# A software-pipelined decoder round in another order on TensorE, VectorE and ScalarE

## What is computed

```python
x = x + L1_attn(LN(x))     # RWKV: k, v, r = shifted mixes @ W; wkv scan over 16 steps;
                           # x += (r * wkv) @ Wo; then channel mix:
                           # x + sigmoid(yr @ Wcr) * (relu(yk @ Wck)**2 @ Wcv)
x = x + L1_xattn(LN(x), context)
    # scores = Q K^T (4 heads, 77 keys); keep the 32 largest; softmax; mean over heads
    # c_t = attn_mean @ V; film: x = n*(1+scale_in)+shift_in
    # y = irfft(rfft(x) * Kf); y = y*(1+scale_out)+shift_out; xt = x + y
    # h = gelu(LN(xt) @ W1 + b1) @ W2 + b2;  LN(xt + h)
x = x + clip(LN(x) @ sign(W) * scale + bias, -100, 100)
```

## Time and profile before

| | us |
|---|---|
| median of 3 runs | 1935.76 |
| lowest and highest run | 1935.62, 1937.24 |
| time of the profiled execution | 1936.92 |
| its span, first to last instruction | 1935.2 |
| TensorE busy in the span | 1686.4 (87%) |
| VectorE busy | 1287.0 (67%) |
| ScalarE busy | 864.3 (45%) |
| GpSimd busy | 605.3 (31%) |

### The profile page before, as it was taken

One profiled execution on the slowest core, in us unless ns is written; L12 is line 12 of the kernel. 1 busy time (PEld: TensorE's weight loads), 2 busy tenths in 40 slices (PEclk: granted clock), 3 DMA queues, 4 the chain that ended last, 5 costly groups with the idle time before them and its releaser, 6 DMA issues.

```text
span 1935.2 us, 26723 instructions
## 1 busy us (share of the span) xinstructions
PE 1686.4 (87%) x8210; PEld 1308.0 (68%) x8210; DVE 1287.0 (67%) x4141; ACT 864.3 (45%) x1675; POOL 605.3 (31%) x984
## 2 busy tenths in 40 slices
PE   5899999992299999982779999999999999999775
PEld 3677777771166677761658778778778778777654
DVE  3567777762148777334478888889888889876642
ACT  1444444440031111114556766667766667754321
POOL 1111111213300000005534445545444544433211
PEclk9899999995699999995789999999999999999987
DMA  9000000006644343425000000000000000000000
GB/s 272 3 1 1 1 1 1 1 1 234 249 137 137 110 119 99 134 77 197 12 6 1 12 12 6 12 6 12 12 12 6 12 6 7 6 6 1 6 6 11
DMA packets 81573, 94.11 MB, mean 49 GB/s; under 512 B 19142, under 2 KB 69527, under 8 KB 81179
## 3 DMA queue, kind: packets, MB, share of 16 engines
q1 hardware_dynamic: 72747, 78.91, 12.7%
q0 software_dynamic: 3072, 8.39, 1.2%
q10 hardware_dynamic: 5616, 5.11, 0.8%
HBM read 71.94 MB, written 20.45 MB: 48 GB/s over the span
## 4 chain that ended last, share of the span: by engine, by line
PE 35%; DVE 13%; ACT 2%; issue 2%; POOL 2%; POOLq 0%; ACTq 0%
PE E_pY L2313 6%; PE E_pK L2204 5%; PE E_pU L2303 4%; PE E_pK L2163 3%; PE E_pY L2151 3%; PE E_pS L2266 3%; PE E_pY L2284 3%; PE E_pU L2275 2%; DVE E_wk L1738 2%; DVE E_ex L1670 2%; DVE E_m L1731 1%; PE E_pY L2163 1%; PE E_pT L2145 1%; DVE E_num L1677 1%; PE E_pY L2214 1%
## 5 line engine op out<-in xcount | busy, mean ns | idle before, releaser
L1222 ACT ACTIVATE F_uT<-F_puT 128x1024 f32<-128x1024 f32 x39 | 39.9, 1024 | 294.3 <-PE F_puT L1282 294.3
L1492 POOL TENSOR_SCALAR E_var<-E_mv 128x2 f32<-128x2 f32 x80 | 34.2, 427 | 355.9 <-DVE E_mv L1607 355.7
L1273 PE MATMUL F_pu<-C_W,F_hT 128*128 x312 | 143.9, 605 | 0.3 <-issue 0.3
L1291 PE MATMUL F_py<-C_W,F_uT 128*128 x624 | 141.2, 379 | 1.2 <-ACT F_uT L1222 1.2
L1291 PEld LDWEIGHTS F_py<-C_W,F_uT 128*128 128x128 f32 x624 | 115.6, 190 | 16.0 <-issue 1.9
L2214 PE MATMUL E_pY<-E_Wcv,E_hid 128*128 128x256 f32 x512 | 118.7, 386 | 3.3 <-issue 3.3
L2303 PE MATMUL E_pU<-E_xT,E_W 128*128 128x256 f32 x512 | 117.7, 385 | 2.3 <-ACT E_xT L2052 2.3
L2313 PE MATMUL E_pY<-E_W,E_hid 128*128 128x256 f32 x512 | 118.1, 379 | 0.0
L2204 PE MATMUL E_pK<-E_cmix,E_Wck 128*128 128x256 f32 x512 | 115.8, 379 | 1.3 <-ACT E_hid L1993 1.3
L2214 PEld LDWEIGHTS E_pY<-E_Wcv,E_hid 128*128 128x128 f32 x512 | 96.0, 192 | 27.8 <-issue 15.6
L2303 PEld LDWEIGHTS E_pU<-E_xT,E_W 128*128 128x128 f32 x512 | 98.7, 193 | 16.7 <-ACT E_xT L2052 2.9
(11 more groups left out here) (402 smaller groups left out, 4353.9 us busy)
## 6 DMA issues: line engine op xcount, KB each, us to landing
F_b<-in_L_ffn_b SPq DMA_DIRECT2D x39, 512.0 KB, 4.4
C_W<-in_L_ffn_W SPq DMA_DIRECT2D x16, 1024.0 KB, 14.0
sorted_x<-zero SPq DMA_DIRECT2D x1, 4992.0 KB, 19.5
F_xs<-sorted_x SPq DMA_DIRECT2D x39, 128.0 KB, 2.4
F_b<-in_L_ffn_b SPq DMA_DIRECT2D x39, 128.0 KB, 3.1
sorted_y<-F_y ACTq DMA_DIRECT2D x39, 128.0 KB, 2.3
out<-E_tB SPq DMA_DIRECT2D x16, 256.0 KB, 2.1
X<-in_x SPq DMA_DIRECT2D x3, 1024.0 KB, 10.7
```

The costliest lines, as they stand in the source:

```text
L1273: last = nc.tensor.matmul(p_u[:, f, :], hT[:, i % 2, kb, :], W1[:, bass.ds(e, 1), kb, f * 512:(f + 1) * 512], start=kb == 0, stop=kb == KD ...
L1291: last = nc.tensor.matmul(p_y[:, 0:D], uT[:, f, :], W2[:, bass.ds(e, 1), f, :], start=f == 0, stop=f == FB - 1)
```

## The change

Only the order of steps changes, on three engines; no step is added or dropped, and GpSimd and the DMA queues keep theirs. Each step issues the same instructions as before.

On VectorE `film` is cut into its halves: half 0 stays at the end of the round, half 1 goes behind `add_network` at the start of the next (where this sequence is called i). `norm_out` goes ahead of `new_maximum` and `scores`; `spectrum` ahead of `take` 0; `scale_out` ahead of `numerator`; `output` ahead of `denominator`; `take` 2 and `take` 3 behind `gated` and `stats_E`, with `residual` between them; `stats_1` ahead of `add_mix`.

On ScalarE `h_1` goes behind the first two `rectify`, `exps_E` behind `context`, and `film` 1 behind `queries`.

On TensorE `values_D` goes ahead of `scores`; half of `channel_out` for rows 1 ahead of `turn_3`; half of `network` for rows 1 ahead of `turn_average`; `turn_E` directly behind `turn_average`; `film` 0 behind the last half of `network`; and `queries_keys` between the two halves of `film`.

```diff
-            def film(j):
-                dve.wait_ge(e["n1"], j + 1)
-                for t in range(2):
-                    dve.wait_ge(e[f"fp{t}"], j + 1)
+            def film(j, t):
+                if t == 0:
+                    dve.wait_ge(e["n1"], j + 1)
+                dve.wait_ge(e[f"fp{t}"], j + 1)
...
@@ VectorE, one round
                 if 0 <= p < B:
                     add_network(p)
+                if 0 <= i < B:
+                    film(i, 1)
                 if t < B:
                     difference(t)
-                if 0 <= j < B:
-                    scores(j)
+                if 0 <= p < B:
+                    norm_out(p)
                 if t < B:
                     new_maximum(t)
-                if 0 <= p < B:
-                    norm_out(p)
+                if 0 <= j < B:
+                    scores(j)
                 if 0 <= c < B:
                     add_channel_mix(c)
-                if 0 <= j < B:
-                    take(j, 0)
                 if 0 <= i < B:
                     spectrum(i)
                 if 0 <= j < B:
+                    take(j, 0)
                     take(j, 1)
-                if t < B:
-                    numerator(t)
                 if 0 <= i < B:
                     scale_out(i)
                 if t < B:
-                    denominator(t)
+                    numerator(t)
                 if 0 <= p < B:
                     output(p)
                 if t < B:
+                    denominator(t)
                     invert(t)
-                if 0 <= j < B:
-                    take(j, 2)
-                if t < B:
                     gated(t)
-                if 0 <= j < B:
-                    take(j, 3)
                 if 0 <= c < B:
                     finish(c)
                     stats_E(c)
+                if 0 <= j < B:
+                    take(j, 2)
                 if t < B:
                     residual(t)
                 if 0 <= j < B:
+                    take(j, 3)
                     average(j)
+                if t + 2 < B:
+                    stats_1(t + 2)
                 if t + 1 < B:
                     add_mix(t + 1)
-                if t + 2 < B:
-                    stats_1(t + 2)
-                if 0 <= j < B:
-                    film(j)
+                if 0 <= j < B:
+                    film(j, 0)
                 if 0 <= c < B:
                     keys(c)
@@ ScalarE, one round
-                if t + 1 < B:
-                    h_1(t + 1)
                 if 0 <= c < B:
                     rectify(c, 0, 0)
                     rectify(c, 0, 1)
+                if t + 1 < B:
+                    h_1(t + 1)
...
-                if 0 <= j < B:
-                    exps_E(j)
                 if 0 <= c < B:
                     square(c, 0)
...
                 if 0 <= j < B:
                     context(j)
+                    exps_E(j)
...
                     film(j, 0)
-                    film(j, 1)
                 if 0 <= c < B:
                     queries(c)
+                if 0 <= j < B:
+                    film(j, 1)
@@ TensorE: channel_out takes the range of blocks that it works off
-            def channel_out(n, c, a):
+            def channel_out(n, c, a, first, end):
...
-                last.then_inc(z["vv" if a else "vv0"], 1)
+                if end == FB:
+                    last.then_inc(z["vv" if a else "vv0"], 1)
@@ TensorE, one round
+                if t < B:
+                    values_D(n, t)
                 if 0 <= j < B:
                     scores(j)
                 if t < B:
-                    values_D(n, t)
                     receptance_D(n, t)
...
                 if 0 <= c < B:
-                    channel_out(n, c, 0)
+                    channel_out(n, c, 0, 0, FB)
+                    channel_out(n, c, 1, 0, FB // 2)
                 if 0 <= i < B:
                     turn_3(n, i)
                 if 0 <= c < B:
-                    channel_out(n, c, 1)
+                    channel_out(n, c, 1, FB // 2, FB)
...
                     network(n, i, 0, 0, FB)
+                    network(n, i, 1, 0, FB // 2)
                 if 0 <= j < B:
                     turn_average(n, j)
-                if 0 <= i < B:
-                    network(n, i, 1, 0, FB // 2)
-                if 0 <= j < B:
-                    film(j, 0)
                 if 0 <= c < B:
                     turn_E(n, c)
                 if 0 <= i < B:
                     network(n, i, 1, FB // 2, FB)
                 if 0 <= j < B:
-                    film(j, 1)
+                    film(j, 0)
                 if 0 <= c < B:
                     queries_keys(c)
+                if 0 <= j < B:
+                    film(j, 1)
```

More of the change, by code:

```diff
@@ L1755, in average @@
                 v.tensor_reduce(am[:], ex[:].rearrange("p t h j -> p t j h"), AX.X, ALU.add).then_inc(e["am"], 1)
-            def film(j):
-                dve.wait_ge(e["n1"], j + 1)
-                for t in range(2):
-                    dve.wait_ge(e[f"fp{t}"], j + 1)
[L1761 to L1764, removed]
+            def film(j, t):
+                if t == 0:
+                    dve.wait_ge(e["n1"], j + 1)
+                dve.wait_ge(e[f"fp{t}"], j + 1)
+                chained(v.tensor_tensor(u[:, t, :], u[:, t, :], p_S[:, 0, 0:D], ALU.mult))
+                v.tensor_tensor(hE[:, j % 2, t, :], hE[:, j % 2, t, :], p_S[:, 1, D:2 * D], ALU.add).then_inc(e["hs"], 1)
+                settled()
+                v.tensor_tensor(u[:, t, :], u[:, t, :], p_S[:, 0, D:2 * D], ALU.add).then_inc(e["u"], 1)
             def spectrum(i):
@@ L1842, in _ @@
                     add_network(p)
+                if 0 <= i < B:
+                    film(i, 1)
                 if t < B:
                     difference(t)
+                if 0 <= p < B:
+                    norm_out(p)
+                if t < B:
+                    new_maximum(t)
                 if 0 <= j < B:
                     scores(j)
-                if t < B:
-                    new_maximum(t)
-                if 0 <= p < B:
-                    norm_out(p)
                 if 0 <= c < B:
                     add_channel_mix(c)
-                if 0 <= j < B:
-                    take(j, 0)
                 if 0 <= i < B:
@@ L1867, in _ @@
                 if t < B:
+                    denominator(t)
                     invert(t)
+                    gated(t)
+                if 0 <= c < B:
+                    finish(c)
+                    stats_E(c)
                 if 0 <= j < B:
@@ L1871, in _ @@
                 if t < B:
-                    gated(t)
+                    residual(t)
                 if 0 <= j < B:
                     take(j, 3)
[L1875 to L1879, removed]
-                if 0 <= j < B:
                     average(j)
+                if t + 2 < B:
+                    stats_1(t + 2)
                 if t + 1 < B:
                     add_mix(t + 1)
-                if t + 2 < B:
-                    stats_1(t + 2)
                 if 0 <= j < B:
-                    film(j)
+                    film(j, 0)
                 if 0 <= c < B:
@@ L2212, in channel_out @@
                     latest(pe, (f["z"], n - 4), (e["Yr"], n - 3), (z["gate2"], c))
-                for fb in range(FB):
+                for fb in range(first, end):
                     last = te.matmul(p_Y[:, a, :], hid[:, fb, a * P:(a + 1) * P], Wcv[:, fb, :],
                                      start=fb == 0, stop=fb == FB - 1)
-                last.then_inc(z["vv" if a else "vv0"], 1)
+                if end == FB:
+                    last.then_inc(z["vv" if a else "vv0"], 1)
             def turn_E(n, j):
```

## The result

The changed kernel is slower. Its median is 1962.81 us (1960.88 to 1968.34, four runs) against 1936.42 (1935.62 to 1937.24, four runs) for the kernel before on the same chip: a ratio of 1.0141 over all the runs, interval 1.0119 to 1.0162. Its profiled execution took 1963.71 us, with a span of 1962.0, 26.8 more than before. TensorE is busy for 1686.8 us of it and VectorE for 1285.8, both within 1.3 us of before: the same work, with more standing still between its parts.

What follows compares the result with a forecast made beforehand. TensorE, busy 57.01 of a 57.88 us round, was taken as the bound. Twelve full rounds at +1.87 plus 3.4 for filling and emptying rounds gave +25.8, forecast 1962 us, range 1945 to 1978.

Steps and rivals of the forecast that it cites:

- The gains: TensorE's waits at `turn_3` (0.3) and `out_product` (0.47) go, -0.77 a round; `project`'s wait stays.
- Item 1: `output` on VectorE ends later, so TensorE's `channel_out` waits for p_Y: +0.39 a round.
- Item 2: `turn_E` directly behind `turn_average` waits for ScalarE's copy out of p_T, starting 0.84 behind instead of 0.22: +0.62.
- Item 3: `film` half 1 waits until half 0 is read; halves 3.72 apart with 3.23 of work: +0.49.
- Item 4: VectorE's chain from `inverse` delays `average`; `turn_average` 0.4 late without contention, bringing the round to +1.07.
- Contention: VectorE products in `finish` and `average` newly overlap GpSimd's: two at 0.4, +0.8 a round.
- full locks: Rival: two newly overlapped VectorE products pay the whole 0.95 each, 2.97 a round, 1975 us; chance 0.14.
- The end rounds: Filling and emptying rounds: round 2 +1.5, round 3 +1.9, rounds 16 to 19 0 give or take 4; together +3.4.
- `film`'s 2: In rounds 16 to 19, `film` halves with only 1.73 ahead lose up to 2 in one round.
- short covers alone: Rival: only TensorE's new short covers cost, `average` in time, no contention; +0.73 a round, 1945 to 1949; chance 0.15.
- Faster: Rival: `turn_E` and `film` 1 find buffers read, new waits 0.1 a round, 1926 us; chance 0.06.
- nothing moves: Rival: new waits and the two removed come out even within 4 us, 1932 to 1940; chance 0.07.

Runs made afterwards that it cites:

- experiment 7: Kernel before plus only half of `channel_out` for rows 1 ahead of `turn_3` and `take` 3 behind `stats_E`: 1926.59 us, ratio 0.994.
- experiment 1: Changed kernel with `numerator` back ahead of `scale_out`: 1979.13 us, ratio 1.0233 to the kernel before.
- experiment 2: Changed kernel with `numerator` back ahead of `scale_out` and `take` 2 back between `invert` and `gated`: 1962.69 us, ratio 1.0127.
- experiment 3: Changed kernel with `numerator` ahead of `scale_out`, `take` 2 between `invert` and `gated`, `h_1` ahead of the first `rectify`: 1953.39 us, ratio 1.0079.
- experiment 4: Changed kernel with TensorE's round end reordered: quarter `network`, `film` 0, `turn_E`, last quarter, `queries_keys`, `film` 1: 1951.93 us, ratio 1.0073.
- experiment 5: Kernel before with only the changed end of TensorE's round and the `film` steps belonging to it: 1954.42 us, ratio 1.0084.
- experiment 6: Changed kernel with `exps_E` back ahead of `square` on ScalarE: 1966.98 us, ratio 1.0152 to the kernel before.

## Why the prediction was right

The forecast was 1962 and the median is 1962.81, on the forecast's own mechanism: new waits of TensorE, and `average` late on VectorE. The mechanism of the full rounds was right; that the total came so close is luck, as the last steps below show. By its steps:

- *The gains.* -0.77 was said, 0.38 + 0.47 = 0.85 is found, and experiment 7 has 0.88 of them alone. `project`'s 0.44 stayed and VectorE's wait moved to `scale_out`, as said (2.91 before, 4.08 now).
- *Item 1*, p_Y for `channel_out`: 0.39 said, 0.27 found.
- *Item 2*, `turn_E`: it starts 1.00 behind `turn_average` where 0.84 was said. The copy ends 0.86 behind (0.80 by the earlier trace rows), and TensorE starts 0.14 after its end (1484.43 less 1484.29), for which the 0.84 left only 0.04.
- *Item 3*, `film` half 1: 3.71 against 3.72. It costs 0.48 beside the work between, as said.
- *Item 4*, `average`: 0.93 late against 0.4 from the chain and 0.8 for contention, 1.2 together; with the contention that is found, 0.36, it would have been 0.76. The other 0.17 are mostly TensorE, which is ready sooner than laid out: 26.97 behind the start of `scale_out` (1482.50 less 1455.53) instead of 27.18. VectorE does have no idle time behind `scale_out`, as laid out. But experiment 1 shows a second bound right behind it: with `numerator` early, `finish` waits 1.70 for `channel_out`. The layout had this (1456.72 against 1456.63 for `gated`). In the changed kernel's own full rounds it costs nothing, since VectorE doesn't wait there.
- *Contention*: the term that was mis-sized, 0.36 instead of 0.8 in a round. L1697 takes 0.67 although L1526 of GpSimd runs beside it, L1701 takes 1.05 instead of 0.69 beside L1526 and L1531, and L1744 takes 0.80 (0.77 before) because `add_x1` (1477.94 + 1.27) is just done. In experiment 1, L1701 falls otherwise against GpSimd and takes 1.72. Which of `finish`'s two products pays was open, and it is the second, with both inputs in SBUF, and not the first, which reads p_Y in PSUM. By the Trainium skill, SBUF — State Buffer, section "Who interferes with whom", that is how it should be: a VectorE instruction with two SBUF inputs contends with a GpSimd instruction that reads SBUF, one with at most one SBUF input outside the 2-port modes doesn't, and the shared port pair is an exclusive lock. The traces agree. They also show what the prediction lacked, the size. It is not a whole GpSimd instruction that is waited for: each time the extra is what was left of GpSimd's instruction when VectorE's began, less 0.13 or 0.14. For L1701 in after 0.50 was left (1470.13 less 1469.63) and 0.36 is paid; in experiment 1 1.16 was left (1293.22 + 1.27 less 1293.33) and 1.03 is paid; for L1677 in before 1.09 was left (1454.67 + 1.72 less 1455.30) and 0.95 is paid. So the term follows from the phase of the two engines, which the prediction replaced by a chance of one half. The *full locks* rival, 1.9 in a round, is out.
- *The end rounds*: 3.4 was said for both ends. Rounds 0 to 3 give +4.0 against +3.4, but not where it was said. Round 2 was to lose 1.5 and is 0.6 shorter: inside the round `turn_average` comes 2.2 later, not 2.8, and behind it 9.76 pass to the next `keys_D` instead of 12.61. Round 3 loses 1.6 of the 1.9 said. Rounds 0 and 1, put at nothing, lose 1.2 and 1.7. In round 0 that is `stats_1`, costed at nothing: it now stands ahead of `add_mix` in a round in which TensorE waits for `add_mix`, 4.41 instead of 3.50 (at 920.11 and 920.26). In round 1 it goes with `h_1`, costed at nothing too: its place is worth 3.7 by experiments 2 and 3, of which 3.0 are `channel_out` at another clock (10.13 instead of 7.14; 10.19 in after and 8.83 in before). TensorE's row of `turn_average` in round 2 of after, against the earlier trace rows:

```profile
1008.63 0.71 PE L2254 MATMUL E_pT<-ident,E_am 128*77 128x128 f32 x2 [11.36 <-DVE E_am L1755]
```

  Rounds 16 to 19 give +5.2 where 0, give or take 4, was said. The step that failed there is `exps_E`: it was covered by half of `channel_out` in a full round, and round 17 has no `channel_out`. `film`'s 2 was right (1.9); the slow `hidden` behind the wait was not thought of.

So no step failed in kind in the full rounds; the terms that failed are the contention, mis-sized at 0.8, and in the end rounds the moves put at nothing: `exps_E`, `h_1` and `stats_1`. The full rounds were over-estimated, 22.4 against 19.1, and the ends under-estimated, 3.4 against 9.2; with the -1.4 in the stages ahead, which the change does not touch, the sum of 25.8 came out 1.0 below the 26.8 found. The sum is nearer than its terms because an error of 3.3 one way and one of 4.4 (5.8 less the 1.4) the other nearly cancel, and that is luck.

The rivals: of *short covers alone* the mechanism is real, and it is most of the loss (experiments 4 and 5), but `average` is late as well. *Faster* and *nothing moves* fail on the 1.00 and the 3.71.

## What to carry over

When a step is moved, ask first whether it enters the chain that the next engine waits for: `numerator` behind `scale_out` did, with 2.62. When a step is moved behind a wait, look at what used to fill that wait: one `take` behind `finish` was a gain here, and two of them, once `numerator` was out of the chain, left VectorE nothing to do while it waits for `channel_out`, and delayed `average`. A tile that is written, copied off and written again needs the copy's time in other work between the two writes; put the work there in pieces as small as the copy (0.86 was enough here). A cover that holds in the full round has to be looked up again in the rounds in which its sequence is missing, and an edit of many moves is best split: here two of them carried all the gain.

## What the runs showed of the hardware

TensorE's clock fell in a full round of experiment 1, in which the engine stood still for 1.42 and then 0.56, close together. The table of stretches, experiment 1, a long round and a usual one:

```profile
1246.00:1252.00 6.00, 5.44 (x18) 3.91 (x17) 2.27 (x5) 1.96 (x4) 4.03 (x8) 0.72 0.02 4
1300.00:1306.00 6.00, 6.00 (x29) 5.28 (x28) 5.76 (x33) 2.16 (x5) 2.57 (x5) 1.00 0.00 1
1306.00:1312.00 6.00, 4.03 (x19) 2.76 (x18) 4.25 (x7) 1.84 (x4) 2.92 (x6) 1.00 0.01 3
```

In the first stretch the granted clock is 0.72, a mean of the 1.2 and the 2.4 GHz level; the eight records of `network` behind the waits take 3.17 instead of 1.89, and the round is 62.02 instead of 60.34. The usual round has the same two waits, 1.41 and 0.56, and keeps 1.00. So waits of this size can cost 1.7 more than themselves, in some rounds and not in others; after's, 0.77 and 0.56, did not: none of its full rounds is longer than 59.74. In round 17 of after, 4.57 of standing still were followed by a `hidden` of 9.38 at a granted clock of 0.74; with 1.16 in experiment 6 it took 7.01 at 1.00. Such a wait has to be priced with what the engine does behind it.
